# Moving the output projection of attention and its residual from slot 8 to slot 9 of the next batch's turn

## The chip, the cores and the metric

The kernel runs on 1 core of one Trainium2 chip. The metric is the device time of one execution, in microseconds (us). Before the change it is 333.81 us, the median of 3 runs (333.81 to 334.44).

## The reference, cut to what matters

Two layers, each a gated cross-attention of 16 heads and a gated feed-forward part, on an input of 4 batches x 512 tokens x 128 channels with 154 context rows. The second layer's feed-forward part is a short recurrence over the batches.

```python
x = x + tanh(g_xattn[0]) * L0_xattn(layernorm(x), ctx)      # 16 heads, softmax over 154 keys, out @ Wo.T + bo
x = x + tanh(g_ffn[0])   * L0_ffn(layernorm(x))             # quantized gate/up/down; its scales are maxima over ALL batches
x = x + tanh(g_xattn[1]) * L1_xattn(layernorm(x), ctx)      # the same attention, causal mask
x = x + tanh(g_ffn[1])   * L1_ffn(layernorm(x))             # c = f*c + i*g over the 4 batches, then h = tanh(x@wo + c@uo + bo)
```

So the feed-forward part of layer 0 can start only when the last batch of its attention is normalized (its scales are maxima over the whole tensor), and each step of layer 1's recurrence needs the normalized output of one batch's attention.

## The kernel before

**Turns and slots.** The program is written out engine by engine; each engine runs its instructions in the order of the code, and semaphores join the engines. A layer's attention goes in turns `i = -1 .. 4`, each of 20 slots (`SLOTS`). In slot `t` of turn `i` TensorE makes score tile `t` of batch `i` (L984; L990 for the keys past 128) and ScalarE takes its exponentials (`exps`, L773). The scores have two PSUM banks in turn (`SRING = 2`; five in turn 3 of layer 0, when the other banks are free), so a score waits for the exponential two tiles back.

**Work ahead.** Beside that, TensorE makes for the next batch the tiles from which the row maxima come (L954, three banks, `MRING = 3`), and VectorE reduces each (`take_top`, L1332). The maxima are split (L1343, L1345) and turned by TensorE in slot 14 (`turn_top`, L967).

**The batch before.** What is left of batch `i - 1` is spread over the slots of turn `i` by three tables, `PE_PLAN`, `ACT_PLAN` and `DVE_PLAN`, which `planned` reads. Shift -1 means the batch before. The steps, in the order in which they depend on each other:

- `tail0`, `tail1` (slots 1, 3; TensorE) finish the weighted values; `div0` to `div3` (slots 3 to 6; VectorE, L1352 to L1365) divide and transpose them into `sb_oT`;
- `wo`, slot 8: on TensorE `project_out` (L1025, four products into the single PSUM bank `ps_misc`, each shown as two instructions), on VectorE `residual` (L1371, reads `ps_misc`, writes `sb_xr`);
- `stat post`, slot 9: VectorE's `norm_stats` (L1292, L1295, writes `sb_mv`); GpSimd follows with `normed` (L627, L629, L637, L644: four instructions, then four that write `sb_xn`);
- `post`, slot 16 in layer 0, slot 18 in layer 1: TensorE's `turn_normed` (L931) transposes `sb_xn` into `ps_misc`, ScalarE copies it out (L745). In layer 0 VectorE takes a maximum of `sb_xn` in slot 16 as well (`amax`, L1313).

In the last batch of a layer VectorE does the normalization itself (L1307) after GpSimd's L629.

**The recurrence of layer 1.** `state` (L1036) and `step` (L1047) on TensorE fill three banks (gates 0 to 2), ScalarE takes the gates (`gate_of`, L782), and VectorE forms the new state (`keep` L1386, `renew` L1393 and L1396). Its four passes are named first to last and have slots of their own in the tables. In turn 3 the slot-8 entries of the pass `first` stand behind `wo`, in turn 4 those of `third`; the closing instructions of VectorE's update (`step` for `first`, `step rest` for `third`) have slot 10, listed behind `stat post`.

Within a slot TensorE does first the score, then the row-maximum tiles, then the entries of the table in the order of the list. The eight output projections are numbered here 1 to 8 in order of time: 1 to 4 in turns 1 to 4 of layer 0, 5 to 8 in turns 1 to 4 of layer 1. Turn 4 has no scores.

```python
def residual(layer, b):
    n = B * layer + b
    dve.wait_ge(misc_full, use["wo", layer, b] + 1)
    dve.wait_ge(xg_r, n + 1)

def turn_normed(kind, layer, b):
    k = norm_no[kind, layer, b]
    pe.wait_ge(xn_r, k + 1)
    fill_misc(pe, (kind, layer, b))
```

## Time and profile before

| | |
|---|---|
| median of 3 runs | 333.81 us (333.81 to 334.44) |
| the profiled execution, its own time | 334.55 us |
| its span, first to last instruction | 332.8 us |
| TensorE busy | 276.4 us (83%) |
| VectorE busy | 251.2 us (75%) |
| ScalarE busy | 190.2 us (57%) |
| GpSimd busy | 136.8 us (41%) |
| granted TensorE clock, mean | 0.954 (full in all stretches with projections) |
| projections 1 to 4 start on TensorE at | 66.68, 86.70, 103.88, 119.94 us |
| projections 5 to 8 start on TensorE at | 249.16, 270.42, 289.97, 311.30 us |

PE is TensorE, DVE VectorE, ACT ScalarE, POOL GpSimd. No engine is full over the span, and each instruction waits in its engine's queue behind those that stand ahead of it. So the table alone does not say what a moved step is worth; that is in the timeline of the engines around each projection, which gives for every instruction its start, how long it took, and how long its engine had been idle before it and for whom.

### The profile page before, as it was taken

What the parts mean: (1) busy time and instruction counts of PE and PEld (TensorE: products, weight loads), DVE (VectorE), ACT (ScalarE), POOL (GpSimd) and SP (SyncE); (2) the same over time, 40 slices, a digit from 0 to 9 for tenths busy, and PEclk for the clock granted to TensorE, in tenths of its full rate; (3) what the DMA queues carried; (4) which work ended last, traced back from release to release, by engine and by line L of the source; (5) the groups of instructions that cost most, each with busy time, mean ns of one, the idle gap of its engine ahead of it and who ended that gap; (6) DMA issues with size and microseconds to landing.
All of it is one profiled execution on the core that took longest, in us unless ns stands there. A gap on an engine that the chain in (4) does not pass through costs nothing. (4 is left out here: it accounts for less than half of the span.)

```text
span 332.8 us, 4411 instructions
## 1 busy us (share of the span) xinstructions
PE 276.4 (83%) x1400; PEld 159.9 (48%) x1400; DVE 251.2 (75%) x538; ACT 190.2 (57%) x303; POOL 136.8 (41%) x274
## 2 busy tenths in 40 slices
PE   1889899899999779986007888889989988999994
PEld 0558555464534255331005776664646644434562
DVE  5689978897987288879989977987688692442834
ACT  1672376566466656769589832436565546664232
POOL 6769893760050311870000259921386307140100
PEclk9979999999999999996557999999999999999999
DMA  7930100020000000000000002220002000000004
GB/s 209 344 120 33 72 33 10 0 102 10 1 8 3 0 0 2 1 0 0 1 0 0 2 0 95 97 102 2 10 0 106 7 0 11 0 1 0 2 1 126
DMA packets 10455, 12.55 MB, mean 38 GB/s; under 512 B 896, under 2 KB 6400, under 8 KB 10432
## 3 DMA queue, kind: packets, MB, share of 16 engines
q1 hardware_dynamic: 10000, 11.80, 10.1%
q10 hardware_dynamic: 432, 0.47, 0.7%
q8 instruction: 11, 0.18, 0.2%
q14 instruction: 12, 0.10, 0.1%
HBM read 4.27 MB, written 1.05 MB: 16 GB/s over the span
## 5 line engine op out<-in xcount | busy, mean ns | idle before, releaser
L773 ACT ACTIVATE sb_pr<-ps_score 128x512 f32<-128x512 f32 (+1 forms) x148 | 82.4, 586 | 55.3 <-PE ps_score L984 46.3
L1332 DVE TENSOR_REDUCE sb_nm<-ps_top 128x3 f32<-128x462 f32 (+2 forms) x168 | 97.1, 626 | 20.4 <-PE ps_top L954 11.9
L954 PE MATMUL ps_top<-sb_Kd,sb_Q 128*128 128x462 f32 (+3 forms) x240 | 71.0, 349 | 2.8 <-DVE sb_nm L1332 1.4
L984 PE MATMUL ps_score<-sb_Q,sb_Kd 128*128 128x512 f32 x119 | 54.8, 471 | 1.5 <-ACT sb_pr L773 1.0
L954 PEld LDWEIGHTS ps_top<-sb_Kd,sb_Q 128*128 128x128 f32 x240 | 43.9, 191 | 14.7 <-DVE sb_nm L1332 8.8
L984 PEld LDWEIGHTS ps_score<-sb_Q,sb_Kd 128*128 128x128 f32 x119 | 22.4, 190 | 32.3 <-ACT sb_pr L773 26.8
L1016 PE MATMUL ps_pv<-sb_pr,sb_V 128*32 128x512 f32 x256 | 34.1, 605 | 0.0
L627 POOL TENSOR_SCALAR sb_var<-sb_mv 128x4 f32<-128x4 f32 x16 | 4.7, 291 | 69.5 <-DVE sb_mv L1295 68.9
L621 POOL TENSOR_SCALAR_AFFINE_SELECT sb_pr<-sb_pr 128x512 f32<-128x512 f32 x16 | 10.5, 659 | 43.3 <-ACT sb_pr L773 43.3
L644 POOL TENSOR_SCALAR sb_xn<-sb_xr,sb_nmean,sb_rstd 128x128 f32<-128x128 f32 x44 | 19.3, 455 | 1.2
L1352 DVE STREAM_TRANSPOSE sb_oq<-ps_pv 128x512 f32<-128x512 f32 x16 | 10.8, 699 | 11.0 <-PE ps_pv L1016 10.9
L498 POOL MEMSET sb_Q<- 128x2048 f32 x1 | 1.8, 1805 | 41.0 <-DVE sb_s L1475 41.0
L629 POOL TENSOR_TENSOR sb_rstd<-sb_var,sb_half 128x4 f32<-128x4 f32 x16 | 17.7, 1107 | 1.3
L522 POOL CAST sb_Kd<-sb_K 32x616 fp32r<-32x616 f32 x20 | 14.1, 704 | 8.5 <-DVE sb_K L1243 7.4
L1016 PE MATMUL ps_pv<-sb_pr,sb_VT 128*32 128x512 f32 (+1 forms) x128 | 14.9, 550 | 0.9 <-ACT sb_pr L773 0.9
L931 PE MATMUL ps_misc<-sb_consts,sb_xn 128*128 128x128 f32 x64 | 10.6, 290 | 5.2 <-POOL sb_xn L644 3.0
L1292 DVE BATCH_NORM_STATS2 sb_stat<-sb_xr 128x6 f32<-128x128 f32 x64 | 13.9, 279 | 1.2 <-DMA sb_xr<-x 1.0
L1083 PE MATMUL ps_misc<-sb_consts,sb_amx 128*128 128x128 f32 x8 | 2.6, 413 | 13.9 <-DVE sb_amx L1402 13.9
L1194 PE MATMUL ps_top<-sb_front,sb_wfT 128*128 128x512 f32 x22 | 11.6, 655 | 2.7 <-ACT sb_uf L831 2.2
L605 POOL TENSOR_TENSOR sb_xg<-sb_xr,sb_bog 128x128 f32<-128x128 f32 x32 | 13.7, 462 | 0.1
L990 PE MATMUL ps_score<-sb_Q,sb_KT 128*128 128x384 f32 (+1 forms) x29 | 12.8, 451 | 0.8 <-ACT sb_pr L773 0.8
L1101 PE MATMUL ps_top<-sb_wfT 128*128 128x256 f32 x30 | 8.9, 449 | 5.2 <-DVE sb_amax L1469 4.7
(180 smaller groups left out, 551.3 us busy)
## 6 DMA issues: line engine op xcount, KB each, us to landing
sb_Q<-sb_qh SPq DMA_DIRECT2D x16, 256.0 KB, 2.3
sb_Q<-sb_ql SPq DMA_DIRECT2D x8, 256.0 KB, 2.3
sb_xr<-x SPq DMA_DIRECT2D x4, 256.0 KB, 7.6
out<-sb_xr SPq DMA_DIRECT2D x4, 256.0 KB, 2.5
sb_wsb<-w SPq DMA_DIRECT2D x1, 704.0 KB, 9.5
sb_wf<-wffn SPq DMA_DIRECT2D x1, 576.0 KB, 9.2
sb_wkr<-wkr SPq DMA_DIRECT2D x2, 256.0 KB, 6.6
sb_Q<-sb_nmT SPq DMA_DIRECT2D x8, 64.0 KB
```

Source lines behind the costliest of these rows:

```text
L522: ins = pool.tensor_copy(Kd[n % 3][q, :, j, :], K4[q, :, b, :])
L605: ins = pool.tensor_tensor(xg[:, n % 2, t, :], xr[:, TT * b + t, :], bog[:, layer, :], ALU.add)
L629: pool.tensor_tensor(rstd[:, k % 4, :], var[:, k % 4, :], half[:, :], ALU.pow).then_inc(rstd_r, 1)
L644: ins = pool.tensor_scalar(xn[:, kind == "post", t, :], xr[:, TT * b + t, :], nmean[:, k % 4, t:t + 1], rstd[:, k % 4, t:t + 1], ALU.add, ...
L773: act.activation(pr[:, k % PRING, q0:T], score_bank(B * layer + b, t)[:, q0:T], ACT.Exp, scale=SCALE).then_inc(exp_r, 1)
L954: ins = pe.matmul(cols[:, c0:c1, :], Q4[n % 3][:, g, P * qt:P * qt + P], Kd[n % 3][:, g, j:j + c1 - c0, 0:keys], start=True, stop=not mask ...
L984: ins = pe.matmul(ps[:, :], Kd[n % 3][:, g, j, 0:P], Q4[n % 3][:, g, :], start=True, stop=True, skip_group_check=True)
L990: ins = pe.matmul(ps[:, q0:T], KT[:, b, t - H, :], Q4[n % 3][:, t - H, q0:T], start=True, stop=(layer == 0), skip_group_check=True)
L1016: ins = pe.matmul(acc[32 * g:32 * g + 32, q0:T], lhs, pr[:, (TILES * n + t) % PRING, q0:T], start=(r in (0, 2)), stop=(r >= 4), skip_group ...
L1194: pe.matmul(fbank[t % FRING][:, :], wfT[:, 3 * (t // 12) + m, :], xq[:, c, :], start=True, stop=True).then_inc(fmm, 1)
L1292: ins = dve.bn_stats(stat6[:, k % 4, t, :], xr[:, TT * b + t, :])
L1332: dve.tensor_reduce(nm[:, (B * layer + b) % 2, :, :].rearrange("p t h -> p (t h)")[:, f0:f0 + heads], top[k % MRING][:, 0:keys * heads].re ...
```

## The change

The entry `wo` goes from slot 8 to slot 9, on TensorE and on VectorE, and `stat post` from slot 9 to slot 10. No instruction is added or removed.

```diff
-PE_PLAN = [(1, "tail0", -1), (3, "tail1", -1), (4, "pre", 2), (7, "pre", 3), (6, "q", 2), (10, "q", 3), (7, "round0", 0), (8, "wo", -1),
+PE_PLAN = [(1, "tail0", -1), (3, "tail1", -1), (4, "pre", 2), (7, "pre", 3), (6, "q", 2), (10, "q", 3), (7, "round0", 0), (9, "wo", -1),
...
-            (7, "q", 2), (8, "wo", -1), (9, "stat post", -1), (13, "top", 1), (14, "post", -1), (16, "amax", -1),
+            (7, "q", 2), (9, "wo", -1), (10, "stat post", -1), (13, "top", 1), (14, "post", -1), (16, "amax", -1),
```

TensorE at projection 1 (turn 1 of layer 0): L1025 is the projection, L984 the score of slot 9, L954 the row-maximum tile of slot 9 (two pieces).

```order
 L954 MATMUL ps_top<-sb_Kd,sb_Q 128x462 x2
-L1025 MATMUL ps_misc<-sb_wsb,sb_oT 128x128 x4
-L984 MATMUL ps_score<-sb_Q,sb_Kd 128x512
-L954 MATMUL ps_top<-sb_Kd,sb_Q 128x154
-L954 MATMUL ps_top<-sb_Kd,sb_Q 128x308
+L984 MATMUL ps_score<-sb_Q,sb_Kd 128x512
+L954 MATMUL ps_top<-sb_Kd,sb_Q 128x154
+L954 MATMUL ps_top<-sb_Kd,sb_Q 128x308
+L1025 MATMUL ps_misc<-sb_wsb,sb_oT 128x128 x4
```

The projection now stands behind one score and one row-maximum tile. Projections 2, 5 and 6 move in the same way; projection 3 moves behind one score; projection 4 keeps its place, since nothing stands between the two slots there.

VectorE at projection 1: L1332 are reductions of the row-maximum tiles, L1371 the residual, L1292 and L1295 the statistics.

```order
-L1332 TENSOR_REDUCE sb_nm<-ps_top 128x3 x3
-L1371 SCALAR_TENSOR_TENSOR sb_xr<-ps_misc,sb_tg,sb_xg 128x512
-L1332 TENSOR_REDUCE sb_nm<-ps_top 128x3
-L1292 BN_STATS sb_stat<-sb_xr 128x6 x4
-L1295 BN_AGGR sb_mv<-sb_stat 128x2 x4
-L1332 TENSOR_REDUCE sb_nm<-ps_top 128x3 x3
+L1332 TENSOR_REDUCE sb_nm<-ps_top 128x3 x4
+L1371 SCALAR_TENSOR_TENSOR sb_xr<-ps_misc,sb_tg,sb_xg 128x512
+L1332 TENSOR_REDUCE sb_nm<-ps_top 128x3
+L1292 BN_STATS sb_stat<-sb_xr 128x6 x4
+L1295 BN_AGGR sb_mv<-sb_stat 128x2 x4
+L1332 TENSOR_REDUCE sb_nm<-ps_top 128x3 x2
```

One more reduction stands ahead of the residual and the statistics, and one fewer behind them. The same holds at projections 2, 5 and 6; at 3, 4, 7 and 8 VectorE's order is unchanged.

TensorE at projection 8 (turn 4 of layer 1): L1047 and L1036 are `step` and `state` of the pass `third`, gate 2; L1058 starts the output.

```order
-L1025 MATMUL ps_misc<-sb_wsb,sb_oT 128x128 x4
-L1047 MATMUL ps_top<-sb_pnT,sb_wsb 128x512
-L1036 MATMUL ps_top<-sb_cst,sb_wsb 128x512
+L1047 MATMUL ps_top<-sb_pnT,sb_wsb 128x512
+L1036 MATMUL ps_top<-sb_cst,sb_wsb 128x512
+L1025 MATMUL ps_misc<-sb_wsb,sb_oT 128x128 x4
 L1058 MATMUL ps_score<-sb_bfo,sb_onesr 128x512 x2
```

The last gate's two products come ahead of the projection. At projection 7 the pair of pass `first` and one score come ahead of it.

## Rows read from the trace of the kernel before

**Rows 1.** The page: busy us (share of the span) and instructions per engine.

```profile
PE 276.4 (83%) x1400; PEld 159.9 (48%) x1400; DVE 251.2 (75%) x538; ACT 190.2 (57%) x303; POOL 136.8 (41%) x274
```

**Rows 2.** Timeline, TensorE, projection 1: start, us taken, what, count.

```profile
66.68 1.06 PE L1025 MATMUL ps_misc<-sb_wsb,sb_oT 128*128 128x128 f32 x8
67.49 0.48 PE L984 MATMUL ps_score<-sb_Q,sb_Kd 128*128 128x512 f32 x1
...
68.06 0.39 PE L984 MATMUL ps_score<-sb_Q,sb_Kd 128*128 128x512 f32 x1
...
74.12 0.60 PE L931 MATMUL ps_misc<-sb_consts,sb_xn 128*128 128x128 f32 x4
```

**Rows 3.** Timeline, VectorE and GpSimd, projection 1; brackets: idle before, for whom.

```profile
66.67 1.18 DVE L1332 TENSOR_REDUCE sb_nm<-ps_top 128x3 f32<-128x462 f32 x2 [0.20 <-PE ps_top L954]
67.78 0.75 DVE L1371 SCALAR_TENSOR_TENSOR sb_xr<-ps_misc,sb_tg,sb_xg 128x512 f32<-128x512 f32 x1
...
72.07 1.79 POOL L644 TENSOR_SCALAR sb_xn<-sb_xr,sb_nmean,sb_rstd 128x128 f32<-128x128 f32 x4
```

**Rows 4.** Timeline, GpSimd, TensorE and VectorE, behind projection 2.

```profile
92.44 1.79 POOL L644 TENSOR_SCALAR sb_xn<-sb_xr,sb_nmean,sb_rstd 128x128 f32<-128x128 f32 x4
...
94.29 0.64 PE L931 MATMUL ps_misc<-sb_consts,sb_xn 128*128 128x128 f32 x4
...
94.26 0.69 DVE L1313 TENSOR_REDUCE sb_amax<-sb_xn 128x1 f32<-128x512 f32 x1 [1.20 <-POOL sb_xn L644]
```

**Rows 5.** Timeline, TensorE and GpSimd, projection 3.

```profile
103.88 1.16 PE L1025 MATMUL ps_misc<-sb_wsb,sb_oT 128*128 128x128 f32 x8 [0.41 <-DVE sb_oT L1365]
...
109.76 1.75 POOL L644 TENSOR_SCALAR sb_xn<-sb_xr,sb_nmean,sb_rstd 128x128 f32<-128x128 f32 x4
...
111.56 0.66 PE L931 MATMUL ps_misc<-sb_consts,sb_xn 128*128 128x128 f32 x4 [0.83 <-POOL sb_xn L644]
```

**Rows 6.** Timeline, VectorE and GpSimd, projection 5.

```profile
252.41 0.38 DVE L1295 BATCH_NORM_AGGREGATE sb_mv<-sb_stat 128x2 f32<-128x6 f32 x4
...
254.08 0.20 POOL L627 TENSOR_SCALAR sb_var<-sb_mv 128x4 f32<-128x4 f32 x1
```

**Rows 7.** Timeline, TensorE and VectorE, projection 6.

```profile
270.42 1.16 PE L1025 MATMUL ps_misc<-sb_wsb,sb_oT 128*128 128x128 f32 x8 [1.10 <-DVE sb_oT L1365]
...
271.61 0.75 DVE L1371 SCALAR_TENSOR_TENSOR sb_xr<-ps_misc,sb_tg,sb_xg 128x512 f32<-128x512 f32 x1 [0.18 <-PE ps_misc L1025]
...
276.86 0.33 PE L967 MATMUL ps_misc<-sb_consts,sb_nms 128*128 128x128 f32 x1 [0.23 <-DVE sb_nms L1345]
```

**Rows 8.** Timeline, VectorE, ScalarE and TensorE, projection 7.

```profile
291.06 0.75 DVE L1371 SCALAR_TENSOR_TENSOR sb_xr<-ps_misc,sb_tg,sb_xg 128x512 f32<-128x512 f32 x1 [4.00 <-PE ps_misc L1025]
...
294.94 0.69 DVE L1396 SCALAR_TENSOR_TENSOR sb_cst<-sb_tmp 128x512 f32<-128x512 f32 x1
...
294.07 2.97 ACT L773 ACTIVATE sb_pr<-ps_score 128x512 f32<-128x512 f32 x5
...
297.87 1.10 PE L1036 MATMUL ps_top<-sb_cst,sb_wsb 128*128 128x512 f32 x2
```

**Rows 9.** Timeline, TensorE and VectorE, projection 8 to the recurrence's last pass.

```profile
311.30 1.16 PE L1025 MATMUL ps_misc<-sb_wsb,sb_oT 128*128 128x128 f32 x8 [0.51 <-DVE sb_oT L1365]
312.29 1.02 PE L1047 MATMUL ps_top<-sb_pnT,sb_wsb 128*128 128x512 f32 x2
313.15 1.02 PE L1036 MATMUL ps_top<-sb_cst,sb_wsb 128*128 128x512 f32 x2
...
312.50 0.75 DVE L1371 SCALAR_TENSOR_TENSOR sb_xr<-ps_misc,sb_tg,sb_xg 128x512 f32<-128x512 f32 x1 [0.68 <-PE ps_misc L1025]
...
314.93 0.69 DVE L1393 SCALAR_TENSOR_TENSOR sb_tmp<-sb_gt 128x512 f32<-128x512 f32 x1 [0.37 <-ACT sb_gt L782]
...
316.40 1.98 PE L1036 MATMUL ps_top<-sb_cst,sb_wsb 128*128 128x512 f32 x4
...
316.97 1.11 DVE L1307 TENSOR_SCALAR sb_xn<-sb_xr,sb_mv,sb_rstd 128x128 f32<-128x128 f32 x4 [0.62 <-POOL sb_rstd L629]
```

## The prediction

> **What bounds the kernel now.** The page comes first: TensorE is busy 276.4 us and VectorE 251.2 of 332.8 [rows 1], so two engines share the load and neither is full. An edit that moves instructions and adds none is then worth what happens to waits, place by place. I went to the eight projections with the timelines of all engines side by side and asked three things at each: what does TensorE wait for in front of the projection; what follows the residual on VectorE and GpSimd; and who meets the end of that chain, the transposition L931 of the normalized batch, in TensorE's queue.
>
> In front of the projection there are gaps: TensorE stands idle for VectorE's transpose `sb_oT` for 0.41 us at projection 3, 1.10 at 6 and 0.51 at 8 [rows 5, 7, 9]. Another score or step fits into those. That is what there is to win.
>
> At the other end of the chain there is almost no room in layer 0. Behind projection 1, GpSimd's last normalization ends at 72.07 + 1.79 = 73.86, and TensorE comes to L931 at 74.12: 0.26 us to spare [rows 2, 3]. Behind projection 2 it ends at 92.44 + 1.79 = 94.23 and TensorE starts at 94.29, with VectorE already standing 1.20 us for the same normalization [rows 4]. Behind projection 3 TensorE waits 0.83 for it [rows 5]. So in layer 0 the chain residual, statistics, GpSimd, L931 ends last or within 0.3 us of it, and the change puts a reduction into that chain.
>
> **The change, projection by projection.** The profiled execution took 334.55 us (span 332.8, and 1.75 around it); the median of the runs is 333.81, 0.74 less. I sum the effects against 334.55 and lay the sum on the median.
>
> *Projection 1.* On TensorE the score and the row-maximum tile that now come first take 68.06 - 67.49 = 0.57 us from start to start. The projection is not waiting for anything there, so it ends 0.57 later, at 66.68 + 1.06 + 0.57 = 68.31, and what follows in TensorE's queue is where it was [rows 2]. VectorE had its residual at 67.78, right behind its reductions. A further reduction costs 1.18 - 0.63 = 0.55 (two take 1.18, one about 0.63 with its tail) and ends at about 68.33; the residual starts at about 68.38, 0.60 later than before [rows 3]. Statistics and GpSimd's instructions do nothing but follow, so `sb_xn` is complete at 74.46 instead of 73.86. TensorE starts L931 0.05 after such an end (109.76 + 1.75 = 111.51, start 111.56) [rows 5], so at 74.51 instead of 74.12: **+0.39**. Behind L931 in that queue stand the scores of slots 17 on and the rounds; TensorE is the full engine there, so I let the loss run through. Bounds: 0 if the next turn had a gap to lose it in, 0.60 if TensorE came to L931 0.2 earlier in the new order.
>
> *Projection 2.* VectorE is again without a gap, the projection is again off the path, and the statistics come one reduction later, 0.55. `sb_xn` ends at 94.78, L931 starts at 94.83 instead of 94.29, and VectorE's `amax`, now at 94.81, pushes the whole weight preparation behind it [rows 4]. TensorE and VectorE are late together by 0.54 and 0.55, and the next turn's transpose `sb_oT` with them. I take **+0.50**, a little less than that, for a short wait that may be eaten on the way; bounds 0.3 and 0.55.
>
> *Projection 3.* TensorE is idle 0.41 in front of it, and one score goes there (together with a row-maximum tile it took 0.57 at projection 1, so alone it is less). The projection starts as before, when `sb_oT` is there, and so do residual, statistics and GpSimd. The scores behind it run up to 0.41 earlier, and TensorE then comes earlier to L931, where it waits 0.83 for GpSimd already [rows 5]. The gain becomes wait: **0**. Bounds: -0.41 if that wait were for something else, 0. *Projection 4* keeps its order: 0.
>
> *Projection 5.* The statistics end at 252.41 + 0.38 = 252.79, but GpSimd takes them up only at 254.08, because in layer 1 it first masks tiles of exponentials [rows 6]. A reduction of 0.55 disappears in 1.29 of cover: **0**. If that cover were gone it would cost up to 0.55.
>
> *Projection 6.* TensorE fills its 1.10 with a score and a row-maximum tile. But the row-maximum stage is held by VectorE here: TensorE waits for the split maxima at 276.86 (0.23). VectorE does the same work in other order, and saves only its own wait for the projection, 0.18, since it has a further reduction to do meanwhile [rows 7]: **-0.18**. Bounds: -0.57 if TensorE's lead counted in full, 0.
>
> *Projection 7.* The projection goes behind two pairs of the recurrence and a score, 0.86 + 0.86 (start to start of such pairs, 313.15 - 312.29) [rows 9] + 0.3: about 2.0 us later. The pairs and gate 2 come earlier, but the exponentials behind them run as a closed train of five in 2.97 us and keep their pace [rows 8], so I give **-0.10**. The price falls on VectorE: it waits for the projection, as it did (4.00), now until 293.1, and the state's update, queued behind residual and statistics, ends 294.94 + 0.69 + 1.6 = 297.2. The next reader, TensorE's `state` at 297.87, still finds it ready [rows 8]. Bounds: -0.86 if the earlier pair counted in full; +0.5 if the update were late by as much as its cover of 0.6 may be off.
>
> *Projection 8.* Here the cover is gone. TensorE no longer waits 0.51; it does the last step and state first. They take 0.86 each [rows 9], so the projection starts at 311.30 - 0.51 + 1.72 less some 0.17 by which such pairs overlap what follows (1.02 against 0.86) = 312.34, 1.04 later than before. The residual follows, from 312.50 to 313.54. VectorE's `step rest` is queued behind residual and statistics. Before, it stood there 0.37 waiting for the gate at 314.93. Now the gate is early and the statistics are late: it starts 1.04 - 0.37 = 0.67 later, 0.72 with the handover that follows statistics. The new state is what TensorE starts with at 316.40 (six products, 1.98 for the first four), and all that follows is TensorE back to back to the output: **+0.72**. The normalization that runs beside it (L1307 at 316.97 plus 1.11, to 318.08) comes 1.04 later, at 319.1, before TensorE's six products from 317.12 are done, so it adds nothing [rows 9]. Bounds: +0.4 if TensorE's overlaps are larger, +1.04 if the normalization decides.
>
> *Sum:* 0.39 + 0.50 + 0 + 0 + 0 - 0.18 - 0.10 + 0.72 = **+1.33**; 335.88 for an execution like the profiled one, 335.14 on the median.
>
> **A rule that speaks otherwise.** The page shows the same 276.4 us of TensorE's work and 251.2 of VectorE's before and after, since no instruction comes or goes [rows 1]. The Trainium skill, page "Perfetto Trace Analysis", section "Identifying Performance Opportunities", says that kernels generally improve by improving the most-contended engine; by it this change, which leaves that engine's work alone, gives 333.81. The waits of 0.41 to 1.20 us in rows 4 to 9 speak against using it for a term of this size, and it is the second rival below.
>
> **The rivals.** *Faster: the filled gaps are the path.* At projections 3, 6 and 8 TensorE loses 0.41 + 1.10 + 0.51 = 2.02 us; if TensorE's queue alone set the end, a part up to all of it would come back, 333.81 - 2.02 = 331.8 at most. It decides if L931 in layer 0 has its data in time after all, that is if the statistics come less than about 0.3 us later. For it: the gaps are real. Against it: L931 waits 0.83 behind projection 3, VectorE 1.20 behind 2, and at 8 the update is queued behind the residual. *The same: layer 0 absorbs its delay.* If the stalls behind projections 1 and 2 are lost in later waits (VectorE's idle 0.20 before a reduction shows that there are some), only the last turn counts: 0.72 - 0.28 = +0.44, 334.25. *More: the rest of the delay shows.* With projections 1 and 2 at their upper ends, 0.60 and 0.55, the gains of 6 and 7 at nothing and 8 at 1.04 the sum is 2.19, 336.0. *That the change does not do what it says* is excluded by the order for seven of the eight; the fourth stays.
>
> **How the numbers follow.** The forecast, with the sum between about +0.9 and +1.8, gets 0.65; more than that 0.08; the second rival 0.20; the first 0.07. A measurement of this kernel can tell about 0.2% from no change, 0.67 us: slower is above 334.48, faster below 333.14. Slower has the first two and a part of the second rival's (its 334.25 lies close under the line), 0.77; the same 0.17; faster 0.06. The predicted time is 335.1. The range of 8 in 10 reaches down to the second rival with some room, 333.9, and up to near the sum of the upper ends, 335.9.
>
> **What would show it.** Right: TensorE idle in front of L931 for GpSimd's `sb_xn` behind projections 1 and 2, some 0.4 and 0.5 us, where there was none, and a longer wait than 0.83 behind projection 3; no idle time of TensorE in front of projections 3 and 8; VectorE's `amax` behind projection 2 later by 0.5 against the scores of that turn; in the last turn L1393 directly behind the statistics without the 0.37, and TensorE idle some 0.7 before the six products of `state`. Wrong: if the distance from projection 1 to projection 3 grows by less than 0.4, layer 0 has cover that I did not see; if the six products start as early against the gate as before, the term of projection 8 falls; if the stretch from projection 6 to the last turn shortens by over 0.8, the gaps were on the path.

## The result: 336.93 us, slower by 0.7%

The changed kernel takes 336.93 us, the median of 8 runs (335.21 to 338.73); the kernel before, run beside it, 334.68 (8 runs, 333.81 to 335.38). The ratio is 1.0070, 95% interval 1.0041 to 1.0098. Slower was forecast, but by less: the time lies above the range, which ended at 335.9. The loss is 2.25 us between these medians where the sum said 1.33. Another 0.87 of the distance to 335.1 lies in the base: the three runs that the sum was laid on, which are the first three of these eight, had a median of 333.81, the eight 334.68.

Two more series of the same kernel gave 1.0058 (1.0030 to 1.0085) and 1.0076 (1.0048 to 1.0103). What stands out in all three is the spread. Of 134 runs of the kernel before, over all series, none took more than 336.4 us (the longest 336.33). Of 23 runs of the changed one 14 did.

### The profile page after: what moved, and what is told of

It reads as the page before. It is cut to its first block and busy times, and to the rows that moved or that the text cites. A ratio compares the mean times of both kernels' runs of the same rounds, so it can differ in the third digit from the quotient of the medians.

```text
span 333.4 us, 4411 instructions
## 1 busy us (share of the span) xinstructions
PE 275.0 (82%) x1400; PEld 159.2 (48%) x1400; DVE 251.2 (75%) x538; ACT 190.4 (57%) x303; POOL 137.8 (41%) x274
## 3 DMA queue, kind: packets, MB, share of 16 engines
HBM read 4.27 MB, written 1.05 MB: 16 GB/s over the span
## 5 line engine op out<-in xcount | busy, mean ns | idle before, releaser
L1332 DVE TENSOR_REDUCE sb_nm<-ps_top 128x3 f32<-128x462 f32 (+2 forms) x168 | 97.1, 627 | 20.2 <-PE ps_top L954 11.5
L954 PE MATMUL ps_top<-sb_Kd,sb_Q 128*128 128x462 f32 (+3 forms) x240 | 69.4, 344 | 3.6 <-DVE sb_nm L1332 1.7
L984 PE MATMUL ps_score<-sb_Q,sb_Kd 128*128 128x512 f32 x119 | 55.6, 475 | 1.7 <-ACT sb_pr L773 1.5
L954 PEld LDWEIGHTS ps_top<-sb_Kd,sb_Q 128*128 128x128 f32 x240 | 43.3, 189 | 14.9 <-DVE sb_nm L1332 8.6
L984 PEld LDWEIGHTS ps_score<-sb_Q,sb_Kd 128*128 128x128 f32 x119 | 22.4, 190 | 32.8 <-ACT sb_pr L773 27.6
L627 POOL TENSOR_SCALAR sb_var<-sb_mv 128x4 f32<-128x4 f32 x16 | 5.3, 332 | 70.2 <-DVE sb_mv L1295 69.6
L931 PE MATMUL ps_misc<-sb_consts,sb_xn 128*128 128x128 f32 x64 | 10.6, 290 | 6.1 <-POOL sb_xn L644 4.0
L1292 DVE BATCH_NORM_STATS2 sb_stat<-sb_xr 128x6 f32<-128x128 f32 x64 | 13.9, 279 | 1.7 <-DMA sb_xr<-x 1.5
```

The source lines that it names most:

```text
L931: ins = pe.transpose(misc[:, P * t:P * t + P], xn[:, kind == "post", t, :], ident[:, :])
L954: ins = pe.matmul(cols[:, c0:c1, :], Q4[n % 3][:, g, P * qt:P * qt + P], Kd[n % 3][:, g, j:j + c1 - c0, 0:keys], start=True, stop=not mask ...
L984: ins = pe.matmul(ps[:, :], Kd[n % 3][:, g, j, 0:P], Q4[n % 3][:, g, :], start=True, stop=True, skip_group_check=True)
L1292: ins = dve.bn_stats(stat6[:, k % 4, t, :], xr[:, TT * b + t, :])
L1332: dve.tensor_reduce(nm[:, (B * layer + b) % 2, :, :].rearrange("p t h -> p (t h)")[:, f0:f0 + heads], top[k % MRING][:, 0:keys * heads].re ...
```

## The profile after

The profiled execution took 335.21 us (span 333.4), the lowest of the eight, 0.66 more than the profiled one of before. The page says no more than it did, in answer to [rows 1]:

```profile
PE 275.0 (82%) x1400; PEld 159.2 (48%) x1400; DVE 251.2 (75%) x538; ACT 190.4 (57%) x303; POOL 137.8 (41%) x274
```

So the reading goes place by place again. In the timelines the first number is the start, the second the time taken, the brackets hold the idle time before and for whom.

Behind projection 1 (timeline of the kernel after, VectorE, TensorE, GpSimd; answers [rows 2, 3]):

```profile
66.40 1.73 DVE L1332 TENSOR_REDUCE sb_nm<-ps_top 128x3 f32<-128x462 f32 x3 [0.19 <-PE ps_top L954]
68.05 0.74 DVE L1371 SCALAR_TENSOR_TENSOR sb_xr<-ps_misc,sb_tg,sb_xg 128x512 f32<-128x512 f32 x1
...
74.13 0.66 PE L931 MATMUL ps_misc<-sb_consts,sb_xn 128*128 128x128 f32 x4 [0.32 <-POOL sb_xn L644]
...
72.33 1.75 POOL L644 TENSOR_SCALAR sb_xn<-sb_xr,sb_nmean,sb_rstd 128x128 f32<-128x128 f32 x4
```

This execution is 0.27 ahead of the one of before when it comes here (66.40 against 66.67); executions differ that much and more at the start. Below, this difference ahead of projection 1 is called the offset of a trace. Against that, L931 starts 74.13 - 74.12 + 0.27 = 0.28 later, and for the reason given: TensorE, never idle there before, now stands 0.32 for GpSimd, and starts 0.05 behind its end at 74.08.

Behind projection 2 (the same, TensorE, VectorE, GpSimd; answers [rows 4]):

```profile
94.86 0.66 PE L931 MATMUL ps_misc<-sb_consts,sb_xn 128*128 128x128 f32 x4 [0.49 <-POOL sb_xn L644]
...
94.83 0.69 DVE L1313 TENSOR_REDUCE sb_amax<-sb_xn 128x1 f32<-128x512 f32 x1 [1.73 <-POOL sb_xn L644]
...
93.05 1.75 POOL L644 TENSOR_SCALAR sb_xn<-sb_xr,sb_nmean,sb_rstd 128x128 f32<-128x128 f32 x4
```

L931 is now 94.86 - 94.29 = 0.57 late, 0.56 more than at projection 1, most of it a wait of 0.49 that was not there. VectorE's wait for the same normalization went from 1.20 to 1.73.

At projection 3 (the same, TensorE; answers [rows 5]):

```profile
104.46 1.16 PE L1025 MATMUL ps_misc<-sb_wsb,sb_oT 128*128 128x128 f32 x8 [0.18 <-DVE sb_oT L1365]
...
112.14 0.66 PE L931 MATMUL ps_misc<-sb_consts,sb_xn 128*128 128x128 f32 x4 [1.06 <-POOL sb_xn L644]
```

The wait in front went from 0.41 to 0.18, the one at L931 from 0.83 to 1.06: the same 0.23, and 0.58 late before and after it. What was gained was handed on as wait. The forecast had no idle time left in front of this projection; 0.18 was. At projection 5 the delay is the same too (L627 at 254.67 against 254.08, 0.59) [rows 6].

At projections 6 and 7 (the same, TensorE and VectorE; answers [rows 7, 8]):

```profile
271.01 1.16 PE L1025 MATMUL ps_misc<-sb_wsb,sb_oT 128*128 128x128 f32 x8
...
272.50 0.72 DVE L1371 SCALAR_TENSOR_TENSOR sb_xr<-ps_misc,sb_tg,sb_xg 128x512 f32<-128x512 f32 x1
...
277.18 0.33 PE L967 MATMUL ps_misc<-sb_consts,sb_nms 128*128 128x128 f32 x1 [0.48 <-DVE sb_nms L1345]
...
293.29 0.75 DVE L1371 SCALAR_TENSOR_TENSOR sb_xr<-ps_misc,sb_tg,sb_xg 128x512 f32<-128x512 f32 x1 [5.94 <-PE ps_misc L1025]
...
297.00 0.69 DVE L1396 SCALAR_TENSOR_TENSOR sb_cst<-sb_tmp 128x512 f32<-128x512 f32 x1
...
298.06 1.10 PE L1036 MATMUL ps_top<-sb_cst,sb_wsb 128*128 128x512 f32 x2
```

L967 is 0.32 late, no longer 0.59: a gain of 0.27. At projection 7 the state's update ends at 297.69, and its reader L1036 at 298.06 does not wait for it; that reader is 0.19 late, another 0.13 gained.

From projection 8 to the six products of `state` (the same, TensorE and VectorE; answers [rows 9]):

```profile
312.54 1.05 PE L1025 MATMUL ps_misc<-sb_wsb,sb_oT 128*128 128x128 f32 x8
313.52 0.72 PE L1058 MATMUL ps_score<-sb_bfo,sb_onesr 2*128 2x512 f32 x2
...
315.19 0.61 PE L1064 MATMUL ps_pv<-sb_wsb,sb_pnT 128*128 128x128 f32 x4
317.06 2.84 PE L1036 MATMUL ps_top<-sb_cst,sb_wsb 128*128 128x512 f32 x6 [1.26 <-DVE sb_cst L1396]
319.74 0.60 PE L931 MATMUL ps_misc<-sb_consts,sb_xn 128*128 128x128 f32 x4
...
313.63 0.75 DVE L1371 SCALAR_TENSOR_TENSOR sb_xr<-ps_misc,sb_tg,sb_xg 128x512 f32<-128x512 f32 x1 [1.61 <-PE ps_misc L1025]
...
315.32 0.38 DVE L1295 BATCH_NORM_AGGREGATE sb_mv<-sb_stat 128x2 f32<-128x6 f32 x4
315.62 0.66 DVE L1393 SCALAR_TENSOR_TENSOR sb_tmp<-sb_gt 128x512 f32<-128x512 f32 x1
```

The projection is 1.24 late, the residual 1.13, L1393 0.69, the six products 0.66. The 0.37 in front of L1393 is gone, as foretold, and TensorE stands 1.26 us in front of the six products, where before it came without a wait. From there to the output everything is 0.66 late.

| place | forecast | in the trace |
|---|---|---|
| projection 1, L931 | +0.39 | +0.28 |
| projection 2, up to L931 | +0.50 | +0.56 |
| projections 3, 4, 5 | 0 | +0.02 |
| projection 6 | -0.18 | -0.27 |
| projection 7 | -0.10 | -0.13 |
| projection 8 | +0.72 | +0.47 |
| sum | +1.33 | +0.93 |

(0.66 late at the end, and 0.27 ahead at the start, make the same 0.93.) So the trace confirms the mechanism of every term, with a sum 0.4 smaller than forecast, while the measured loss is 0.9 larger. Something is missing that this execution does not show. That is the question of the experiments.

One sign of being wrong came up by its letter: from the start of projection 1 to the start of projection 3 the trace grew by 37.57 - 37.20 = 0.37, less than 0.4. But projection 1 itself now starts 0.48 later (66.89 against 66.68, and the offset), and the distance counts that as its beginning. From the point ahead of both, the delay at projection 3 is 0.58 + 0.27 = 0.85, so it does not show cover in layer 0.

## The experiments

In several of them part of the change is undone by one line in `planned`. A condition on the layer and the turn, where it is true, takes one slot off, that is, puts both entries back; here `layer == 1`, and other conditions below are named alone:

```diff
-        at += LATER.get((what, shift), 0) if layer == 1 and i < B else 0
+        at += (LATER.get((what, shift), 0) if layer == 1 and i < B else 0) - (what in ("wo", "stat post") and layer == 1)
```

### Both kernels again

The kernels before and after, unchanged.

> The kernel before, once more. Theory O (order alone): its executions lie close together, 333.8 to 335.4 us, and the moved kernel lies 0.7 to 1.0 us above, whatever the clock. Theory C (clock): the moved kernel's time is 2.3 us longer at the median because its executions have stretches at half TensorE clock that this kernel's have not; then the mean granted clocks here are 0.954 to 0.960 in all executions, and the moved kernel's go down to 0.948.

Measured: 334.31 (333.72 to 335.49), ratio 0.9996 (0.9982 to 1.0009).

> The changed kernel, once more. Theory O: 0.7 to 1.0 us above the kernel before in each comparison, spread under 0.5 us. Theory C: a spread of up to 3.5 us, the long executions with a mean clock near 0.948, and in the trace of one a stretch at half clock outside the feed-forward part of layer 0, with the projections' turns longer there. Between projection 1 and projection 3 the trace grows by 0.8 against the kernel before, from projection 6 to 8 it shrinks by 0.4, and behind projection 8 it grows by 0.46, under either.

Measured: 336.28 (334.73 to 338.06), ratio 1.0058 (1.0030 to 1.0085). Four runs lie at 334.73 to 335.19, one at 336.28, four at 337.15 to 338.06. The profile is that of the run with 336.28. Its order is that of the first trace of after up to the six products; then it differs. TensorE's timeline, and the granted clock from 316 to 320 us (the columns are the length of the stretch, then busy us and instructions of PE, PEld, DVE, ACT and POOL, then PEclk, of which 1.00 is 2.4 GHz and 0.50 is 1.2 GHz):

```profile
314.59 0.61 PE L1064 MATMUL ps_pv<-sb_wsb,sb_pnT 128*128 128x128 f32 x4
316.46 4.54 PE L1036 MATMUL ps_top<-sb_cst,sb_wsb 128*128 128x512 f32 x6 [1.26 <-DVE sb_cst L1396]
320.83 0.60 PE L931 MATMUL ps_misc<-sb_consts,sb_xn 128*128 128x128 f32 x4
```

```profile
316.00:320.00 4.00, 3.54 (x5) 1.61 (x6) 1.51 (x5) 0.00 (x0) 1.28 (x1) 0.61 0.01 2
```

The first trace of after has in the same stretch:

```profile
316.00:320.00 4.00, 2.94 (x9) 1.46 (x10) 2.08 (x6) 0.00 (x0) 1.80 (x2) 1.00 0.01 2
```

The idle time in front of the products is 1.26 in both. In the second the clock then falls to its lower level for most of the six products: 4.54 instead of 2.84 us, 1.70 later at the end, on a path where TensorE runs back to back from there to the output. This is theory C's extra stretch, and it has a place.

### One layer alone

The condition is `layer == 1` (only layer 0 moved) and `layer == 0` (only layer 1 moved).

> Moved in layer 0 alone (projections 1 to 3), layer 1 as before. Theory O: +0.8 us (0.3 at projection 1, 0.5 at projection 2, TensorE idle for GpSimd in front of L931 behind both), and nothing beyond. Theory C: +0.8 from the order and, if the idle time in layer 0 is what lowers the clock, executions of 337 us and more here and not with layer 1 moved.

Measured: 335.11 (334.53 to 336.37), ratio 1.0023 (1.0006 to 1.0040), no run above 336.4. In the trace the delay against before grows by 0.28 up to L931 behind projection 1 and to 0.81 behind projection 2, as in the full change:

```profile
74.74 0.66 PE L931 MATMUL ps_misc<-sb_consts,sb_xn 128*128 128x128 f32 x4 [0.28 <-POOL sb_xn L644]
...
95.44 0.66 PE L931 MATMUL ps_misc<-sb_consts,sb_xn 128*128 128x128 f32 x4 [0.47 <-POOL sb_xn L644]
```

> Moved in layer 1 alone (projections 5 to 8), layer 0 as before. Theory O: +0.1 us (-0.3 at projection 6, -0.1 at 7, +0.5 at 8). Theory C: the same in the trace, and executions of 337 us and more here and not with layer 0 moved, if it is layer 1's order that lowers the clock.

Measured: 335.51 (333.79 to 337.08), ratio 1.0025 (1.0007 to 1.0043). The trace has -0.27, -0.12 and +0.47 at projections 6, 7 and 8: by order alone this kernel is 0.08 slower, 1.0002. The runs lie in two groups, five at 333.79 to 334.73 and seven at 335.49 to 337.08; the profile came from the lower one and has full clock at the end. The kernel before has such an upper group too, but a smaller one: 9 of the 32 runs beside these are at 335.12 or more, 7 of 12 here. So layer 0 pays by order, and layer 1 by something that strikes a part of the executions more often than before.

### Projection 8

The condition is `(layer, i) == (1, B)` (all moved but projection 8) and `(layer, i) != (1, B)` (projection 8 alone moved).

> All projections moved but projection 8 (the last batch of layer 1), which stays at its old place. Theory O (order alone): +0.28 behind projection 1, +0.50 behind 2, -0.30 at 6, -0.10 at 7, nothing behind 8: 0.4 us above the kernel before, with as little spread between executions as that one. Theory E (the end's clock): what the moved kernel has beyond that comes from TensorE idling before the products into `state` behind projection 8, so without that move no execution lies more than some 1.5 us above the median of before. Theory G (gaps anywhere): the new idle stretches in layer 0 set off half-clock stretches as well; then executions at 336.5 to 338 remain.

Measured: 335.12 (334.82 to 336.86), ratio 1.0016 (0.9999 to 1.0033); two of 12 runs above 336.4. The clock behind projection 8 is full. The profiled run, 336.86, has two other stretches at the lower level, 38 to 42 us and 218 to 222:

```profile
38.00:42.00 4.00, 4.00 (x14) 3.55 (x15) 3.75 (x7) 1.50 (x3) 3.00 (x13) 0.59 0.34 131
...
218.00:222.00 4.00, 3.53 (x10) 2.75 (x11) 2.44 (x4) 0.28 (x1) 1.58 (x4) 0.60 0.30 109
```

Against the trace of before its delay grows by 0.7 over the first and by 1.1 over the second. The first lies ahead of projection 1 and the second ahead of projection 5, about the start of turn 0 of either layer, where TensorE's instructions stand in the old order; they may belong to the spread that the kernel before has as well. The first trace of the kernel before has such a stretch further ahead, from 18 to 22 us (granted clock 0.58).

> Only projection 8 (the last batch of layer 1) is moved, the seven others stand as before. Theory O: 0.46 us above the kernel before. Theory E (the end's clock): two groups of executions, one 0.5 above before, the other 1.5 to 1.7 above, where TensorE runs at half clock behind projection 8 and the last batch's recurrence is 1.1 to 1.2 longer. Theory G: as theory O, and the slow executions are found with the moves in layer 0 instead.

Measured: 336.92 (335.03 to 337.81), ratio 1.0044 (1.0025 to 1.0064); 7 of 12 runs above 336.4. One moved projection out of eight gives most of the loss, though its order is worth 0.46, 1.0014. The profile, of the run with 335.85, shows the half clock at the same place:

```profile
316.27 4.29 PE L1036 MATMUL ps_top<-sb_cst,sb_wsb 128*128 128x512 f32 x6 [1.26 <-DVE sb_cst L1396]
```

Theory E stands, theory G does not: undoing projection 8 takes most of the high runs away, moving it alone brings them. The two kernels ran side by side and cost the same by order, about 0.5 in either trace, and their medians differ by 1.80.

### The wait at L931 in layer 0

On TensorE alone, the transposition behind projections 1 to 3 comes one slot later:

```diff
-        at += LATER.get((what, shift), 0) if layer == 1 and i < B else 0
+        at += LATER.get((what, shift), 0) if layer == 1 and i < B else (what == "post" and layer == 0 and i < B and plan is PE_PLAN)
```

> The moved kernel, with the transposes of the normed residual (L931 behind projections 1 to 3) one slot later in layer 0 too, so that TensorE no longer stands in front of them for GpSimd; nothing else is changed. If the +0.28 and +0.50 behind projections 1 and 2 are that wait, both go and the kernel is 0.8 below the moved one (about 0.1 above before where the end's clock is undisturbed); if something else behind the move made them, it is within 0.2 of the moved one.

Measured: 335.95 (334.85 to 336.76), ratio 1.0022 (1.0007 to 1.0037). TensorE's timeline behind projections 1 and 2:

```profile
74.73 0.60 PE L931 MATMUL ps_misc<-sb_consts,sb_xn 128*128 128x128 f32 x4
...
94.94 0.66 PE L931 MATMUL ps_misc<-sb_consts,sb_xn 128*128 128x128 f32 x4
...
120.14 1.16 PE L1025 MATMUL ps_misc<-sb_wsb,sb_oT 128*128 128x128 f32 x8 [0.18 <-DVE sb_oT L1365]
```

The waits of 0.32 and 0.49 are gone. At projection 4 this execution is 0.20 late (120.14 against 119.94); it was 0.11 late in front of projection 1. So 0.09 is left of the 0.85 that layer 0 cost, and the cause forecast for it, TensorE standing in front of L931, is shown. The end still has its half clock in this trace (the six products take 4.54), so the gain cannot be read from the ratio alone.

### The state ahead of the residual

In the last turn, VectorE's two closing operations of the state stand ahead of the residual:

```diff
-            (7, "q", 2), (9, "wo", -1), (10, "stat post", -1), (13, "top", 1), (14, "post", -1), (16, "amax", -1),
+            (7, "q", 2), (9, "step rest", "third"), (9, "wo", -1), (10, "stat post", -1), (13, "top", 1), (14, "post", -1), (16, "amax", -1),
             (10, "step", "first"), (19, "step", "second"),
-            (7, "step half", "third"), (10, "step rest", "third"), (19, "step", "last")]
+            (7, "step half", "third"), (19, "step", "last")]
```

> The moved kernel, with VectorE's two state operations (L1393, L1396) of the last turn ahead of the residual of projection 8 rather than behind its statistics. Theory O: the two operations (about 0.9 together) fall into the 1.6 us in which VectorE waits for projection 8, so that `state` is there when TensorE wants it; the +0.46 of projection 8 goes, the rest stays, some 0.4 above before. Theory E: with TensorE's idle time before the `state` products gone, the executions with half clock at the end go as well. Against both: the second operation waits for the sigmoid of ScalarE; if that is late the residual is late behind it, and nothing is won.

Measured: 336.09 (335.04 to 336.89), ratio 1.0034 (1.0018 to 1.0051), 5 of 12 runs above 336.4. The objection held. VectorE's and TensorE's timelines:

```profile
314.91 0.69 DVE L1393 SCALAR_TENSOR_TENSOR sb_tmp<-sb_gt 128x512 f32<-128x512 f32 x1 [1.44 <-ACT sb_gt L782]
...
316.24 0.74 DVE L1371 SCALAR_TENSOR_TENSOR sb_xr<-ps_misc,sb_tg,sb_xg 128x512 f32<-128x512 f32 x1
...
321.31 0.66 PE L931 MATMUL ps_misc<-sb_consts,sb_xn 128*128 128x128 f32 x4 [1.49 <-DVE sb_xn L1307]
```

The products into `state` come without a wait, but the residual now stands behind L1393, which waits 1.44 for ScalarE's gate, and TensorE waits 1.49 for the last normalized batch instead. From projection 8 to the end 0.64 is lost by order, where it was 0.46. The profiled run, 336.83, is itself one of the five high ones, and its clock behind projection 8 is full. It has the lower level in two stretches ahead of projection 1:

```profile
18.00:22.00 4.00, 3.84 (x9) 2.00 (x10) 2.55 (x11) 3.17 (x8) 2.93 (x2) 0.57 0.13 50
38.00:42.00 4.00, 3.90 (x13) 3.22 (x13) 3.72 (x8) 1.20 (x2) 3.00 (x13) 0.58 0.36 138
```

So it comes to projection 1 with an offset of 1.13, and the last products of the output (L1218) start 2.29 after those of before: 1.16 by order. That is the whole loss of this kernel at the median too, 336.09 against 334.88. Shifted by 1.16, 14 of the 35 runs of before that stand beside it would lie above 336.4, much the same share as 5 of 12. So this kernel, in which TensorE does not stand idle in front of the six products, loses nothing beyond its order.

### The idle time, filled with products of two rows

The bias products of the output are issued twice, the second time into TensorE's 1.26 us:

```diff
-                            outputs_bias()
+                            outputs_bias(); outputs_bias()
```

> The moved kernel once more, beside the next three. Theory E (order, and the end's clock in a part of the executions): executions in groups, the lower some 0.9 above the kernel before and the upper 1.2 to 1.5 above that; median 1.6 to 2.2 above before.

Measured: 337.24 (335.76 to 338.62), ratio 1.0076 (1.0048 to 1.0103). The profile is of the lowest run, with full clock at the end; the end is 1.03 late against before after an offset of 0.17.

> The moved kernel, with TensorE's four products of the output bias (L1058, 0.9 us together) issued twice, the second time into the 1.26 us in which it waits for `state` behind projection 8; the second set starts its sums afresh, so the output doesn't change. Theory E, and idle time as what lets the clock fall: TensorE idles 0.3 instead of 1.26 there, `state` is not later, no half clock behind projection 8, and the kernel is 0.8 to 1.3 below the moved one, some 0.9 above before (order alone). If the clock falls there for another reason (two rows of 128 are no load, or the stretch is set off elsewhere), it is as the moved one. If the products delay TensorE, it is slower.

Measured: 336.50 (335.43 to 338.53), ratio 1.0062 (1.0040 to 1.0084).

> Projection 8 alone moved, with the same four products a second time in TensorE's 1.26 us. Against 1.0044 of before without them: theory E with idle time as the cause expects 0.46 above before, 1.0014, and no execution in the upper group; otherwise 1.0044 again.

Measured: 336.76 (334.51 to 337.60), ratio 1.0050 (1.0029 to 1.0071). Nothing was won: 14 of the 19 runs of the two kernels lie above 336.4. TensorE's timeline with projection 8 alone moved:

```profile
314.43 0.61 PE L1058 MATMUL ps_score<-sb_bfo,sb_onesr 2*128 2x512 f32 x2
314.89 0.61 PE L1058 MATMUL ps_pv<-sb_bfo,sb_onesr 2*128 2x512 f32 x2
...
316.93 4.54 PE L1036 MATMUL ps_top<-sb_cst,sb_wsb 128*128 128x512 f32 x6 [0.34 <-DVE sb_cst L1396]
```

The idle time is 0.34, and the clock falls all the same. So idle time of TensorE as the timeline shows it, theory E's cause, is not all of it. The bias products are of two rows (2*128 in the timeline), unlike the others there; the next pair of runs puts other products in their place. The profile of the moved kernel filled in this way (338.53, the longest of its series; its six products take 4.51) shows what the highest runs are made of, the lower level at the end and near 38 us as well (and, as in the trace of before, near 18):

```profile
38.00:42.00 4.00, 3.90 (x12) 3.10 (x12) 3.72 (x8) 1.19 (x2) 3.06 (x13) 0.60 0.39 145
...
320.00:324.00 4.00, 4.00 (x14) 2.00 (x14) 1.11 (x4) 0.27 (x1) 0.00 (x0) 0.73 0.01 2
```

### The idle time, filled with products of 128 rows

The eight products of batch 0's output (L1064, as long together as the bias products) are issued once more, ahead of the bias products that start those sums afresh:

```diff
-                pe.wait_ge(pvx, 2 * 2 * B)
+                pe.wait_ge(pvx, 2 * 2 * B); outputs_x(0)
```

> Projection 8 alone moved, with the eight products of batch 0's output (L1064, 128 rows, 0.9 us together) issued once more ahead of the bias products that start those sums afresh, so the output doesn't change. The bias products used before have 2 rows. Theory L (TensorE's load up to the `state` products, in products of all 128 rows, keeps the clock; products of 2 rows are none): no half clock behind projection 8, 0.46 above before, ratio 1.0014, no execution beyond some 336.5. Theory T (something in the order of the products there, not idle time, sets it off): half clock as with the 2-row products, 1.004 to 1.005.

Measured: 334.44 (334.07 to 335.79), ratio 1.0005 (0.9986 to 1.0024), no run above 336.4.

```profile
312.45 0.61 PE L1064 MATMUL ps_score<-sb_wsb,sb_pnT 128*128 128x128 f32 x4
312.90 0.61 PE L1064 MATMUL ps_pv<-sb_wsb,sb_pnT 128*128 128x128 f32 x4
...
316.08 2.84 PE L1036 MATMUL ps_top<-sb_cst,sb_wsb 128*128 128x512 f32 x6 [0.36 <-DVE sb_cst L1396]
```

> The moved kernel with the same 128-row products once more in TensorE's 1.26 us. Theory L: order alone, 0.9 above before with no half clock behind projection 8 (executions from 335.2 to 336.8, the upper ones by the half-clock stretch near 38 us, which lies ahead of every projection). Theory T: as the moved one, 1.9 to 2.5 above.

Measured: 335.36 (334.64 to 336.29), ratio 1.0021 (1.0002 to 1.0039), no run above 336.4; the six products take 2.84 there too, and the end is 0.12 late after an offset of -0.75, 0.87 by order. The medians differ by 1.03. The clock is full in both traces, and the loss that is left is that of the order. The idle time is the same as with the two-row products (0.36 and 0.34), and so is the length of what fills it, 1.0 us. These products use all 128 rows; they are also eight of 128 columns where the others are four of 512, and stand ahead of the first bias products, not behind. Theory L stands, but that it is the rows which count was not tried apart from the rest.

Both traces are of runs in the lower half of their series; that the clock kept up in the other runs as well is read from their times alone. With projection 8 alone, five of the twelve runs lie at 335.34 to 335.79, where the kernel before has such runs too (5 of 23 at 335.43 or more); where these five lose their time was not seen. The two-row runs come from another chip than these, but the moved kernel had its half clock on this one as well (the first repeat).

### The idle time, made in the kernel before

No projection is moved; the bias products and batch 0's go behind the last L931:

```diff
-                        if (layer, i, slot) == (1, B, 10):
+                        if (layer, i, slot) == (1, B, 17):
                             outputs_bias()
                             outputs_x(0)
```

> The kernel before, all projections at their old places, but the bias products and those of batch 0's output (2.05 us together) are issued behind the last L931 rather than behind projection 8, so that TensorE idles some 2 us in front of the products into `state`, with VectorE as before. Order alone: up to 2.05 later at the end, less what the wait for the last normed batch hides (0.1 or so): 1.9 above before. Idle time lets the clock fall (theory L): in a part of the executions 1.2 to 1.7 more, and the half clock to be seen in a trace behind projection 8. Theory T: no half clock there, one group of executions.

Measured: 337.76 (336.73 to 339.12), ratio 1.0087 (1.0057 to 1.0117).

```profile
311.95 1.16 PE L1025 MATMUL ps_misc<-sb_wsb,sb_oT 128*128 128x128 f32 x8 [0.51 <-DVE sb_oT L1365]
...
317.06 4.54 PE L1036 MATMUL ps_top<-sb_cst,sb_wsb 128*128 128x512 f32 x6 [2.23 <-DVE sb_cst L1396]
```

The projection is where it was, TensorE stands 2.23 us in front of the six products, and they take 4.54. Projection 8 is 0.65 late in this trace and the output 4.50: of the 3.85 between them 1.70 is the clock, the rest, 2.15, the products that now come late. The half clock needs no moved projection, only the missing work. That refutes theory T, which had none here.

### Only what the order gains

The condition is `(layer == 0 or i == B)`: projections 5, 6 and 7 alone are moved.

> Only projections 5, 6 and 7 moved (the first three of layer 1); layer 0 and projection 8 stand as before. Theory O: 0.28 to 0.30 gained at projection 6, 0.10 to 0.12 at 7, nothing at 5, nothing lost elsewhere: 0.4 below the kernel before, ratio 0.9988. If the gain is given back behind (the recurrence waits for something else), within 0.1 of before.

Measured: 334.69 (333.49 to 335.72), ratio 0.9995 (0.9978 to 1.0013). The trace has the gain: 0.90 late in front of projection 6, 0.53 at projection 8 and at the end, 0.37 won. With full clock throughout, 1.0 - 0.37 / 334.7 = 0.9989 lies in the interval, and so does 1. No version here is measurably faster than the kernel before.

## Why the prediction was right and wrong

The last two columns set the median above that of the kernel before, run beside it, against the order's part of it. That part is read from the trace, good to about 0.1: how much later than in the trace of before the last products of the output start, less the trace's offset (from VectorE's last `sb_oT` ahead of projection 1, L1365), and less what a lower clock took from the six products and, in one trace, near 218 us. For the first trace of after it is 327.21 - 326.55 + 0.26 = 0.92:

```profile
326.55 1.88 PE L1218 MATMUL ps_pv<-sb_wsb,sb_cst 128*128 128x512 f32 x4
...
327.21 1.88 PE L1218 MATMUL ps_pv<-sb_wsb,sb_cst 128*128 128x512 f32 x4
```

| kernel | six products of `state` in its trace, us | runs above 336.4 us | median above before, us | order, us |
|---|---|---|---|---|
| before | 2.84, 2.84 | 0 of 134 | | |
| after, three series | 2.84, 4.54, 2.84 | 14 of 23 | 2.25, 1.81, 2.53 | 0.9, 0.8, 1.0 |
| projection 8 alone | 4.29 | 7 of 12 | 2.04 | 0.5 |
| layer 1 alone | 2.84 | 1 of 12 | 1.04 | 0.0 |
| after, L931 later | 4.54 | 3 of 12 | 1.07 | 0.2 |
| after, filled with 2 rows | 4.51 | 6 of 8 | 1.79 | 1.0 |
| 8 alone, filled with 2 rows | 4.54 | 8 of 11 | 2.05 | 0.5 |
| before, TensorE idle 2.23 | 4.54 | 6 of 6 | 3.43 | 2.1 |
| layer 0 alone | 2.84 | 0 of 12 | 0.64 | 0.7 |
| all but projection 8 | 2.84 | 2 of 12 | 0.24 | 0.5 |
| 5, 6 and 7 alone | 2.84 | 0 of 12 | -0.02 | -0.3 |
| after, state ahead of the residual | 2.74 | 5 of 12 | 1.21 | 1.2 |
| after, filled with 128 rows | 2.84 | 0 of 12 | 1.03 | 0.9 |
| 8 alone, filled with 128 rows | 2.84 | 0 of 12 | 0.11 | 0.4 |

From the moved kernel down to the row with 2.23 us, TensorE stands idle in front of the six products, for 1.26 us or more or with two-row products in part of that time; these kernels lose 0.8 to 1.6 us more than their order. The six in the lower rows have no such idle time, or 128-row products in it, and lie within 0.3 of their order.

**What failed.** The step is projection 8, and in it the sentence that all that follows the new state "is TensorE back to back to the output: +0.72". The delay was priced as a shift of the six products, each as long as before. But the shift opened an idle stretch of 1.26 us in TensorE's queue (some 0.7 was forecast, as a sign to look for and at no price of its own), and behind it most of the six products run at 1.2 instead of 2.4 GHz in a part of the executions. That costs 1.45 to 1.70 us each time, with nothing behind it to hide it. Of the six traces that have the 1.26, three show it; the other three are of the lowest runs or the lower group of their series. The order's 0.93, with 1.70 in a part of the runs, gives 0.9 to 2.6; the three series have 2.25, 1.81 and 2.53 between medians. The highest runs, at 338 and more, can be made of that and the stretch near 38 us, which is none of projection 8's doing. The upper end of the range took in larger terms of order, and no term of the clock at all; the table of the profile had even noted the full clock in all stretches with projections, and the step took that for given.

**Projection 1** was right in place and cause, 0.28 for 0.39. The residual was 0.54 late, not 0.60, and the end of `sb_xn` 0.49 (74.08 against 73.86, and the offset). TensorE also came to L931 some 0.19 earlier (a score shorter in its queue, L967 at 72.47 against 72.93, less the offset), which shows as wait and not as loss. **Projection 2** was right, 0.56 for 0.50; nothing of it was eaten on the way. Moving L931 one slot later took both away.

**Projections 3, 4 and 5** were right: a gain of 0.23 in front of projection 3 turned into 0.23 of wait behind it.

**Projection 6** was undersized, -0.27 for -0.18, and **projection 8** oversized in its order, +0.47 for +0.72, both for one reason. An instruction of VectorE that follows without a wait, and does not read what the one just ahead of it wrote, starts about 0.08 before that one's end: L1371 at 272.50, though the reductions ahead of it last until 272.58; L1393 at 315.62, though L1295 lasts until 315.70. (One that does read it starts behind its end, as L1396, at 316.31 against 316.28.) So removing a wait of 0.18 gives 0.26, and the wait of 0.37 that projection 8's delay could use up was worth 0.45. And the projection itself takes 1.05 instead of 1.16 when TensorE comes to it without idle time, which makes its own delay of 1.04 one of 0.93 for the residual: 0.93 - 0.45 = 0.48.

**Projection 7** was right: -0.13 for -0.10, and the update is in time for its reader. The 1.6 by which it was to be late came from no row: it ended at 297.69 and not at 297.2, and its cover was 0.37, not 0.6.

**The base.** The sum was made against one execution and laid on the median of three runs, 333.81. That median was at the low edge of the kernel's runs (333.6 to 336.3). In ratios, forecast 1.0040 stands against 1.0070 (1.0041 to 1.0098): nearer than 335.1 against 336.93 looks.

**The rivals.** "The filled gaps are the path" is refuted, and yet not without a grain: projections 5 to 7 alone gain 0.37 in their trace, though not in their times (0.9995). "Layer 0 absorbs its delay" is refuted by the run with layer 0 alone, 1.0023. "More: the rest of the delay shows" has the size nearly right and the cause wrong. By the rule of the Trainium skill weighed there (page "Perfetto Trace Analysis", section "Identifying Performance Opportunities"), read as one on the busiest engine's work alone, nothing should have changed. The trace has 0.93 us from waits, with the same instructions on every engine.

**What stays open** is which executions get the half clock. The same instructions with the same idle time of 1.26 us ran at 2.4 GHz in one trace and at 1.2 in the next. The Trainium skill, page "TensorE: Matmul & The Clock Gate", section "Part 1: The HAM clock gate (the "warmup" mystery)", says that the chip's look at TensorE's activity runs free of the kernel's start; traces that differ at the start by some tenths of a us and then at the end by 1.7 agree with that, but no run here set that phase. Nor was it tried what lowers the clock near 18, 38 or 218 us, in stretches whose instructions the change leaves where they were.

## What to carry to other kernels

Price a step that is moved later by the slack of its consumer, to be read as the distance between the end of the last writer and the start of the reader: 0.26 us behind projection 1 and 0.06 behind 2 were all there was, and of two delays of 0.5 to 0.6 the rest showed, 0.28 and 0.56. When a move opens idle time on TensorE in front of a burst that lies on the path, price the burst at the lower clock as well, and if the idle time cannot be closed, put products that may be done twice into it, as the 128-row ones here and not the two-row ones, or look for a place of the step that leaves it closed. Compare medians of many runs beside each other; a base of three runs can be off by as much as the effect.

## What the runs showed of the hardware

Not expected: with products of two rows in TensorE's queue and 0.34 us of idle time left, the clock fell in both traces; with products of 128 rows that take the same time, and 0.36 left, it did not in either (the rows are not the only difference between them). Six products of 512 columns then took 4.54 and 4.51, or 2.84 us. Behind 1.26 us of idle time it fell in three traces of six, and behind 2.23 in the one there is; both traces of the kernel before, with no idle time there, have the full clock. An "idle before" on VectorE understates what removing it is worth, by 0.08 us here, where the instruction behind the wait does not read the one ahead of it. And the eight instructions of a projection took 1.05 to 1.11 us when TensorE came to them without standing still, and 1.16 when it had stood, if only for 0.14.
